# First row gathers of both expert stages issued inside the dense blocks, in a two-layer gated cross-attention and mixture-of-experts kernel

## What is computed

```python
# layer 0: 64 experts, each token goes to its best 8, capacity 256 per expert
shared = silu(gu[:, :1024]) * gu[:, 1024:] @ shared_down_w        # gu = x @ shared_gate_up_w
shared = shared * sigmoid(x @ shared_gate_w)
w, idx = top_k(softmax(x @ gate_w), 8)
out_e  = silu(x_e @ up_e[:, :256]) * (x_e @ up_e[:, 256:]) @ down_e # rows x_e of expert e
y      = sum over a token's 8 experts of w * out_e
x      = x + tanh(g_ffn[0]) * (y + shared)
# layer 1: 8 experts, each token goes to its best 2, hidden width 2048
moe    = sum over a token's 2 experts of w * (gelu(x @ ew1_e + eb1_e) @ ew2_e + eb2_e)
x      = x + tanh(g_ffn[1]) * (x + mlp(x) + moe)                     # x here normalised
```

## Time and profile before

| what | value |
|---|---|
| median of 3 runs | 2277.45 us (2274.29 to 2281.68) |
| time of the profiled execution | 2282.3 us |
| its span | 2280.6 us, 39537 instructions |
| PE busy | 2115.8 us (93% of the span) |
| DVE, ACT, POOL busy | 1286.1, 1027.9, 522.7 us |
| mean TensorE clock granted | 0.966 of full speed |
| dense block of layer 0 ends | about 691.2 us into the span |
| dense block of layer 1 ends | about 1869.5 us into the span |

### The profile page before, as it was taken

The page is one execution under the profiler, slowest core; times in us unless marked ns, Lnnn a source line. Parts: engine busy times, 40 slices in busy tenths (PEclk is TensorE's granted clock), DMA queues, the critical chain, the costliest instruction groups (busy, mean ns, idle before and its releaser), DMA issues. The chain is left out here.

```text
span 2280.6 us, 39537 instructions
## 1 busy us (share of the span) xinstructions
PE 2115.8 (93%) x13342; PEld 1495.0 (66%) x13343; DVE 1286.1 (56%) x2758; ACT 1027.9 (45%) x2377; POOL 522.7 (23%) x501
## 2 busy tenths in 40 slices
PE   6999999998997999999669999999989979999998
PEld 3777777776953444444347777777769436777775
DVE  4677777766671222222266777777650117777776
ACT  2466666655221111111125666666553006566655
POOL 3000000002353555455330000000013002322331
PEclk9999999997998999999879999999989989999999
DMA  7001011010144999998540000000121226765661
GB/s 245 29 32 33 32 33 32 7 77 30 38 194 146 343 312 338 334 330 254 117 165 29 28 28 27 28 28 1 76 100 53 50 103 254 262 212 206 231 227 26
DMA packets 64525, 290.22 MB, mean 127 GB/s; under 512 B 10403, under 2 KB 10573, under 8 KB 45061
## 3 DMA queue, kind: packets, MB, share of 16 engines
q1 hardware_dynamic: 44660, 249.44, 29.6%
q0 software_dynamic: 19728, 38.97, 7.9%
HBM read 259.82 MB, written 34.97 MB: 129 GB/s over the span
## 5 line engine op out<-in xcount | busy, mean ns | idle before, releaser
L728 ACT ACTIVATE probs<-ps,less_max 100x360 f32<-100x360 f32 (+1 forms) x384 | 212.3, 562 | 163.4 <-DVE less_max L582 89.6
L1568 PE MATMUL pgu<-ring,xT 128*128 x560 | 266.9, 599 | 6.0 <-issue 2.5
L714 ACT ACTIVATE pTs<-pt 128x300 f32<-128x300 f32 x512 | 189.5, 426 | 125.1 <-PE pt L476 124.1
L1568 PEld LDWEIGHTS pgu<-ring,xT 128*128 128x128 f32 x560 | 99.9, 191 | 113.1 <-issue 112.4
L476 PE MATMUL pt<-ident,probs 100*128 100x100 f32 (+1 forms) x1152 | 137.0, 256 | 28.5 <-ACT pTs L714 26.5
L1926 DVE TENSOR_TENSOR ws_low<-w,ws_high 128x2048 fp32r<-128x2048 f32 x63 | 143.1, 2292 | 24.2 <-ACT ws_high L1857 24.2
L476 PEld LDWEIGHTS pt<-ident,probs 100*128 100x128 f32 (+1 forms) x1152 | 116.2, 141 | 58.8 <-issue 35.9
L349 PE MATMUL po<-first 128*128 128x362 f32 (+1 forms) x768 | 145.6, 339 | 2.8 <-PEq L184 2.3
L353 PE MATMUL pp<-first 128*128 128x512 f32 x576 | 146.1, 402 | 2.3 <-DVE first L377 2.3
L353 PE MATMUL po<-first 128*128 128x512 f32 (+1 forms) x576 | 145.0, 400 | 0.0
L349 PE MATMUL pp<-first 128*128 128x360 f32 (+1 forms) x768 | 143.3, 335 | 1.4 <-DVE kT_low L371 1.2
(11 more groups left out here) (302 smaller groups left out, 4212.2 us busy)
## 6 DMA issues: line engine op xcount, KB each, us to landing
ring<-in_l_ew SPq DMA_DIRECT2D x64, 1536.0 KB
w<-in_l_ew SPq DMA_DIRECT2D x64, 1024.0 KB, 8.4
xnT<-in_ctxT SPq DMA_DIRECT2D x14, 1444.0 KB, 6.8
first<-in_l_up SPq DMA_DIRECT2D x2, 4096.0 KB, 13.9
b<-in_l_eb SPq DMA_DIRECT2D x8, 1024.0 KB, 4.7
moe_sum<-zrow SPq DMA_DIRECT2D x2, 2048.0 KB, 13.1
wd<-in_l_down SPq DMA_DIRECT2D x2, 2048.0 KB, 8.1
xn_rows<-mid SPq DMA_DIRECT2D x16, 200.0 KB
```

The costliest lines, as they stand in the source:

```text
L714: act.activation(pTs[:, g % 2, j, 3 * half:3 * half + 3, :].rearrange("k c q -> k (c q)"), pt[:, half, 0:3 * S], ACT.Copy).then_inc(t_out, 1)
L728: act.activation(probs[g % 2 * HPC + j][:, k0:k1], ps[j][0:S, 0:k1 - k0], ACT.Exp, bias=less_max[:, g, seg, j:j + 1], scale=-1.0 if masked ...
L1568: last = pe.matmul(pgu[p][:, :], xT[p][:, c, :], wgu[c], start=c == 0, stop=c == DC - 1)
```

## The change

In both layers the gathers of the first rows are issued in `dense_and_route`: two in layer 0 (both buffers of the first pair), one in layer 1. POOL waits there for `slot_token` (`token_ready`, new), copies the index column (`index_first`) and issues the DMA. In layer 0 the rows go into two buffers of their own (`xg_first`), which lie where `eq` and its neighbours lay and are cleared by POOL once the routing has ended (`slots_ready`), ahead of `with_weights`; the experts' POOL list then begins with the gathers of tiles 2 and 3, which wait for no transpose. In layer 1 the experts use the buffer and index of the early gather itself. In layer 1 PE's two table transposes stand ahead of the 13th down product instead of behind the 14th, and DVE's two table instructions ahead of its work on the 14th. SP no longer waits at the block's end until the initial sums have landed; POOL waits for it in the expert block (`sum_begun`), ahead of the first addition.

```diff
         if swiglu:
-            at_tile = env.after_xnT + before_it([P, K, 3, NS])
+            with ExitStack() as later:
+                second, *env.xg_first = [later.enter_context(nc.sbuf_tensor(env.name("after"), s, dt)) for s, dt in (
+                    ([P, K, 3, NS], F32R), ([P, D], F32), ([P, D], F32))]
+            at_tile = env.after_xnT + [second]
...
                 for t in range(G):
                     begin_sum(t)
-                sp.wait_ge(sum_begun, 16 * G)
                 sp.wait_ge(env.rows_out, 16 * B)
...
+                def first_rows(p):
+                    pool.tensor_copy(env.index_first[p][:, :], env.slot_token[:, p:p + 1]).then_inc(index_ready, 1)
+                    pool.wait_ge(index_ready, p + 1)
+                    pool.sem_inc(passed, 1)
+                    bound = dict(bounds_check=T - 1, oob_is_err=False) if swiglu else {}
+                    pool.indirect_dma_start(
+                        out=env.xg_first[p][:, :], out_offset=None, in_=env.xn_rows[:, :],
+                        in_offset=bass.IndirectOffsetOnAxis(ap=env.index_first[p][:, 0:1], axis=0), **bound)\
+                        .then_inc(env.x_in[p], 16)
                 if swiglu:
+                    pool.wait_ge(slots_ready, 1)
+                    pool.sem_inc(passed, 1)
+                    for p in range(2):
+                        pool.memset(env.xg_first[p][:, :], 0.0).then_inc(x_clear, 1)
                     for t in range(G):
                         with_weights(t)
+                    pool.wait_ge(x_clear, 2)
+                    pool.sem_inc(passed, 1)
+                    pool.wait_ge(env.rows_out, 16 * B)
+                    pool.sem_inc(passed, 1)
+                    pool.wait_ge(token_ready, 1)
+                    pool.sem_inc(passed, 1)
+                    for p in range(2):
+                        first_rows(p)
...
+                if not swiglu:
+                    pool.wait_ge(env.rows_out, 16 * B)
+                    pool.sem_inc(passed, 1)
+                    pool.wait_ge(token_ready, 1)
+                    pool.sem_inc(passed, 1)
+                    first_rows(0)
...
                         n = hf * G + t
+                        if not swiglu and n == NDH * G - 2:
+                            pe.wait_ge(table_in, 16)
+                            for a in range(2):
+                                last = pe.transpose(turned_table[:, a, :], table[:, :, a], env.ident[0:NS, 0:NS])
+                            last.then_inc(table_mm, 1)
...
-                if not swiglu:
-                    pe.wait_ge(table_in, 16)
-                    for n in range(2):
-                        last = pe.transpose(turned_table[:, n, :], table[:, :, n], env.ident[0:NS, 0:NS])
-                    last.then_inc(table_mm, 1)
...
                     if not swiglu:
+                        if n == NDH * G - 1:
+                            dve.wait_ge(table_mm, 1)
+                            dve.tensor_copy(env.slot_token[:, 0:NS], turned_table[:, 0, :]).then_inc(token_ready, 1)
+                            dve.tensor_scalar(env.slot_weight[:, 0:NS], turned_table[:, 1, :], gate, None, ALU.mult)
                         dve.wait_ge(down_mm, n + 1)
...
-                    link(dve.tensor_copy(env.slot_token[:, 0:NS], padding[:, :]))
+                    dve.tensor_copy(env.slot_token[:, 0:NS], padding[:, :]).then_inc(token_ready, 1)
+                    dve.wait_ge(token_ready, 1)
...
# experts_swiglu, POOL (the two memsets of xg stay)
+                pool.sem_inc(index_ready, 2)
...
                 for p in range(2):
-                    fetch(p, p)
-                for p in range(2):
-                    fetch_next(1, p)
+                    fetch(2 + p, p)
+                pool.wait_ge(env.sum_begun, 16 * G)
+                pool.sem_inc(passed, 1)
                 for p in range(2):
                     fetch_next(2, p)
                     add_rows(0, p, True)
# experts_swiglu, PE: the first two transposed tiles come from env.xg_first
-                    rows_turned(1 - p, (i + p) * 16 + 16)
+                    rows_turned(1 - p, (i + p) * 16 + 16, env.xg_first if first else xg)
...
-                rows_turned(0, 16)
+                rows_turned(0, 16, env.xg_first)
# experts_gelu, POOL
-        index_now, xg = sb("index_now", [P, 1], U32), sb("xg", [P, D])
+        index_now, xg, x_in = env.index_first[0], env.xg_first[0], env.x_in[0]
...
-                fetch(0)
+                pool.sem_inc(index_ready, 1)
                 fetch_next(1)
+                pool.wait_ge(env.sum_begun, 16 * G)
+                pool.sem_inc(passed, 1)
                 fetch_next(2)
                 add_rows(0, True)
```

More of the change, by code:

```diff
@@ L913, in dense_and_route @@
         slot_mm = sem("slot_mm")
-        shapes_ready, rows_back, sum_begun = sem("shapes_ready"), sem("rows_back"), sem("sum_begun")
+        token_ready, index_ready, x_clear = sem("token_ready"), sem("index_ready"), sem("x_clear")
+        env.x_in = [sem(f"x_in{p}") for p in range(2 if swiglu else 1)]
+        shapes_ready, rows_back, env.sum_begun = sem("shapes_ready"), sem("rows_back"), sem("sum_begun")
         NP_ = FC * 2
@@ L962, in begin_sum @@
                     new = OLD_ROWS if t == G - 1 else 0
-                    sp.dma_start(env.moe_sum[0][t * P:t * P + P - new, :], acc[new:P, t, :]).then_inc(sum_begun, 16)
+                    sp.dma_start(env.moe_sum[0][t * P:t * P + P - new, :], acc[new:P, t, :]).then_inc(env.sum_begun, 16)
                 if not swiglu:
@@ L1400, in _ @@
                                                   in1=padding[:, :], op0=ALU.add, op1=ALU.add))
-                    link(dve.tensor_copy(env.slot_token[:, 0:NS], padding[:, :]))
+                    dve.tensor_copy(env.slot_token[:, 0:NS], padding[:, :]).then_inc(token_ready, 1)
+                    dve.wait_ge(token_ready, 1)
                     link(dve.tensor_copy(padding[:, :], slot_sums[:, 1, :]))
                     link(dve.tensor_tensor(env.slot_weight[:, 0:NS], slot_sums[:, 2, :], padding[:, :], ALU.add))
-                else:
-                    dve.wait_ge(table_mm, 1)
-                    dve.tensor_copy(env.slot_token[:, 0:NS], turned_table[:, 0, :])
-                    dve.tensor_scalar(env.slot_weight[:, 0:NS], turned_table[:, 1, :], gate, None, ALU.mult)
 def experts_swiglu(nc, env, w_expert):
@@ L1440, in experts_swiglu @@
         ring_in, w_ready = env.ring_in, sem("w_ready")
-        x_in = [sem(f"x_in{p}") for p in range(2)]
+        x_in = env.x_in
         added, sum_at_ready = [sem(f"added{p}") for p in range(2)], sem("sum_at_ready")
@@ L1545, in _, with rows_turned @@
                 n_pairs = pairs_of(pe)
-                def rows_turned(p, arrived):
+                def rows_turned(p, arrived, rows=xg):
                     pe.wait_ge(x_in[p], arrived)
                     for c in range(DC):
-                        last = pe.transpose(px[:, c, :], xg[p][:, c * P:(c + 1) * P], ident[:, :])
+                        last = pe.transpose(px[:, c, :], rows[p][:, c * P:(c + 1) * P], ident[:, :])
                     last.then_inc(x_mm, 1)
@@ L1699, in experts_gelu @@
         w_in = [sem(f"w_in{q}") for q in range(NCH)]
-        b1_in, b2_in, x_in, added = sem("b1_in"), sem("b2_in"), sem("x_in"), sem("added")
+        b1_in, b2_in, added = sem("b1_in"), sem("b2_in"), sem("added")
         sum_at, sum_at_ready, y_biased = sb("sum_at", [P, 1], U32), sem("sum_at_ready"), sem("y_biased")
@@ L2056, in routing_tables @@
             env.tile_buffer = table("tile_buffer", [1, TILES0], I32)
+            env.index_first = [table(f"index_first{p}_", [P, 1], U32) for p in range(2 if layer == 0 else 1)]
+            if layer == 1:
+                env.xg_first = [table("xg_first", [P, D])]
             env.slot_token, env.slot_weight = table("slot_token", [P, SLOTS0 // P], U32), table("slot_weight", [P, SLOTS0 // P])
```

## The result

The changed kernel takes **2270.88 us** in the median of 13 runs (2267.26 to 2275.29), the kernel before 2281.68 in as many (2274.29 to 2285.04). The ratio is 0.9955, with a 95% interval of 0.9944 to 0.9966, so the change gives 0.45%, about 10.3 us. The median of before stands 4.2 us above the one that the forecast started from. The forecast time, 2271.8, fits by luck, for that reason: its gain, 5.6 us, was too small by nearly half.

A forecast was written before the change was run, and what follows sets the result against it. PE, busy 93% of the span, was taken as the bound, with time to gain only in its gaps ahead of each expert stage: 1.1 us (layer 0) + 4.5 (layer 1) = 5.6, from 2277.45 to 2271.8 us, range 2264 to 2277.

The forecast's parts named there:

- the hold is short: Rival for both layers: POOL's drain waits for landing and little more, 4.3 us; gain 9.6 us, 2267.9 us; chance 0.22.
- I take 7.2 us: Both dense blocks' ends: POOL's drain ends 7.2 us behind the last gather's start, bounds 3.7 and 9.4.
- rival 1: Same as "the hold is short", chance 0.22; it held that the 9.4 us behind layer 1's scatters may be mostly queue.
- rival 2: Both layers: no hold, POOL's drain ends with the gather instruction's recorded end; gain 12.7 us, 2264.8 us; chance 0.15.
- a gain of 1.1 us: Layer 0's expert start: PE starts at 697.0 against 698.14, 1.1 us sooner, between -1.1 and +4.6.
- I count no gain from: Layer 0's expert start: PE still idles some 8 us, so its granted clock is as low as before; gain 0.
- 0.4 us later: End of layer 1's dense block: POOL decides, and the release comes 0.4 us later, between 0.7 sooner and 2.6 later.
- POOL early, SP's limit: Layer 1's release, early bound: POOL is done early and SP sets the release, 0.7 us sooner.
- about 0.6: Layer 1's dense block: the table transposes moved ahead of a product delay what follows by about 0.6 us.
- `pu` gains 4.6: Layer 1's expert start: ACT waits for the first weight chunk, not the rows; first `pu` at 1879.7, 4.6 us sooner.
- Next in line is `b1`: Layer 1's expert start: `b1`, landing 13.9 us behind its issue, limits `ph` to 1887.5, a gain of 4.5 us.
- Rival 3: Both layers: POOL's hold grows with what it has in flight, twice 7.2 us; 8.8 us slower, 2286.3 us; chance 0.05.

The follow-up runs named there:

- experiment 5: Changed kernel with layer 0's last two additions as plain writes: 2265.75 us; with a POOL drain added ahead of both layers' last additions: 2259.77 us.
- experiment 2: Changed kernel with SP's wait for the landing of the sum rows put back at the block's end: ratio 0.997 to the kernel before.
- experiment 6: Changed kernel with three idle PE products ending layer 0's dense block: ratio 0.995; with one early layer 0 gather and PE's gap filled by idle products: 2263.67 us.

## Why the prediction was right or wrong

The time fell inside the range and near the forecast, the latter by luck (the kernel before measured 4.2 us higher, and the gain was 4.7 larger than forecast). What happened is the case called "the hold is short" (9.6 us), not the forecast's. Step by step:

- **"So the question is when the release comes"**, and that in layer 0 POOL's drain decides: right, 690.04 to 690.22.
- **"I take 7.2 us"** for POOL's drain behind the last gather's start. This is the step that failed. It measured 2.77 us in layer 0 and 4.05 in layer 1. The lower end, 3.7, was not low enough either, since the second gather lands in 2.64 us. Two of the drains that it was sized from stand behind 142 and 31 indirect DMAs, and what a drain needs behind the landing grows with these. Both also began behind the landing, where it is twice as much for each DMA as for a drain that begins ahead of it, as those behind the gathers do (experiment 5). The third was a long landing, not a hold, as rival 1 had suspected. I took "2.7 to 4.3 us behind" the landing as the property of one DMA, when the difference between the two drains of the earlier trace rows already spoke against a constant. The Trainium skill's section that rival 2 rested on (Perfetto Trace Analysis, "DMA Instruction — SWDGE (GPSIMD)") puts the recorded end at the last descriptor written, and rival 2 let POOL's drain end there, which would be 688.32. The drain went on 1.72 us beyond, to just past the landing. So neither the forecast nor rival 2 holds: a drain waits for landing, and little more after few DMAs.
- **Layer 0, "a gain of 1.1 us"**: 5.36 at `px`, above the upper bound of 4.6. What stood there otherwise was right: the copy, 3.6 us to the second gather (3.57), 1.1 us from release to PE (1.01), and nothing from SP's wait (experiment 2).
- **"I count no gain from" the clock**: in the two traces the stretch behind the first `px` took 0.98 us more than before, but in the other kernels with the same lists it took from 1.0 less to 0.3 more than before. So neither gain nor loss is shown. Keeping the clock up would be worth 1.4 to 3.5 (experiment 6).
- **Layer 1, the release "0.4 us later"**: it is 1.24 sooner from the anchor, less 0.5 for the transposes, thus 0.7 sooner, the end of the bound called "POOL early, SP's limit". Experiment 2 confirms that SP sets it: 1.2 us with its wait back.
- **The transposes, "about 0.6"**: 0.5.
- **ACT waits for `w`, `pu` gains 4.6**: 6.1 measured (6.64 - 0.5). Of the 1.5 above the forecast 0.9 is the release, which was to come 9.27 us from the anchor and came at 8.38, and 0.5 the first chunk, in 5.0 us behind the release and not 5.5.
- **"Next in line is `b1`", `ph` gains 4.5**: 4.5 measured (5.03 - 0.5). The limit was named rightly, but the number was met by two errors that cancel: the release was 0.9 us sooner than forecast, and `b1` landed 14.9 us behind its issue in place of 13.9.
- **The sum**: 9.8 us in the trace against 5.6, of which 4.1 are layer 0's. At the first `px`, where the hold acts, it is 4.3 (5.36 against 1.1). Layer 1's forecast term was met, by the two errors just named.
- **Rival 3**, "The hold grows with what POOL has in flight", with a loss of 8.8 us, didn't come, although the growth with the number is real: 0.66 us behind 15 indirect DMAs. Most of the hold is the landing.

## What to carry to other kernels

Ahead of a block's end ask of each engine when its drain ends. For POOL behind indirect DMAs that is the landing of the last one, and on top something that grows with the number since the last drain (0.04 us each if the drain begins ahead of the landing, 0.08 if it begins behind it, up to about 30). The last gather should thus be the earliest possible, and only what the next block's first instruction needs. A drain put ahead of the last DMA, where POOL waits anyway, moves the rest out of the kernel's end. And before sizing a wait from another place of a trace, look at what differs between two examples there: here the count, and whether the landing came ahead of the drain.

## What the runs showed that was not expected

- A drain of POOL behind 140 indirect DMAs takes 3.91 us though everything has landed. A second drain 0.2 us behind it takes 0.05. One more gather in the block adds 0.08 us. A drain that begins while the last DMA is still under way ends only 1.2 us behind the landing, after 29 as after 139 of them.
- With 4.1 us of idle PE in place of 9.5 the granted clock falls to 1.2 GHz just the same. When it falls differs between traces with the same lists, from 2.1 to 5.4 us behind PE's last work in the dense block (in the latter case the first transposes of the next block have already run). Thirteen identity products of 128x128 and one of 128x512, all in idle time, keep it at 2.4 GHz in all three kernels that have them, and the stretch takes 5.19 us in each in place of 6.6 to 8.6.
- The experts' stage of layer 0 takes from 420 to 428 us for instructions that are nearly the same on each engine. That is more than what most edits of this study do, and it is open.
